# Turning the exponentials of local attention one step later, with the engines' orders moved to match

## The reference

```
q, k, v = split(shift_token(x) @ wqkv)
q = l2norm(q) * qs ; k = l2norm(k) * ksc ; q, k = rotary_xpos(q, k)
sim = einsum(q * 8, look_around(k))          # 64 queries against 128 keys
sim = where(i < j or i > j + 64 or j == -1, -max, sim)
o = softmax(sim) @ look_around(v)
x = x + o @ wo
h = layernorm(shift_token(x)) * lg + lb
a, g = split(h @ w1 + b1) ; x = x + (a * gelu(g)) @ w2 + b2
```

## Time and profile before

| | |
|---|---|
| median of 3 runs | 1146.2 us (1145.76 to 1147.83) |
| the profiled execution | 1146.11 us, of which its span 1144.2 |
| granted TensorE clock, mean | 0.978 of full speed |
| TensorE busy | 1070.0 us, 94% of the span |
| VectorE busy | 836.6 us, 73% |
| ScalarE busy | 632.1 us, 55% |
| GpSimd busy | 751.2 us, 66% |

### The profile page before, as it was taken

One profiled execution on the slowest core, in us unless ns is written; L12 is line 12 of the kernel. 1 busy time (PEld: TensorE's weight loads), 2 busy tenths in 40 slices (PEclk: granted clock), 3 DMA queues, 4 the chain that ended last, 5 costly groups with the idle time before them and its releaser, 6 DMA issues. The chain is left out here.

```text
span 1144.2 us, 22954 instructions
## 1 busy us (share of the span) xinstructions
PE 1070.0 (94%) x8344; PEld 665.8 (58%) x8344; DVE 836.6 (73%) x1521; ACT 632.1 (55%) x998; POOL 751.2 (66%) x511
## 2 busy tenths in 40 slices
PE   6884899999999999999999999789999898999988
PEld 4452455555555555555555555756777795777678
DVE  6994666666766666676666663889998689888867
ACT  2442356666666566656655654036666455666554
POOL 3662466767677776867677677389996337666526
PEclk9996799999999999999999999899999999999999
DMA  8899621524215243151242101001111100111111
GB/s 260 275 270 352 155 54 48 111 71 88 75 47 113 48 91 84 50 116 43 75 94 66 48 11 47 10 10 32 42 33 32 26 2 19 32 33 33 34 26 36
DMA packets 82625, 88.48 MB, mean 77 GB/s; under 512 B 32037, under 2 KB 65361, under 8 KB 82513
## 3 DMA queue, kind: packets, MB, share of 16 engines
q1 hardware_dynamic: 82512, 87.01, 29.7%
HBM read 53.04 MB, written 24.24 MB: 68 GB/s over the span
## 5 line engine op out<-in xcount | busy, mean ns | idle before, releaser
L873 DVE CUSTOM_DVE_ANT_0 junk<-psum,alibi 128x1024 bf16<-128x1024 f32 x256 | 313.1, 1223 | 200.7 <-PE psum L929 191.9
L845 ACT ACTIVATE E<-psum,keybias_sb 128x1024 f32<-128x1024 f32 x256 | 274.7, 1112 | 229.0 <-PE psum L953 215.8
L775 POOL TENSOR_TENSOR sum_p<-sum_p,E 128x1024 f32<-128x1024 f32 x96 | 232.4, 2421 | 89.3 <-ACT E L845 84.6
L965 PE MATMUL psum<-E,V 128*64 128x512 f32 x1024 | 248.2, 606 | 0.0
L929 PE MATMUL psum<-KH,QH 64*128 64x512 f32 x512 | 118.8, 459 | 12.8 <-PEq L274 7.3
L965 PEld LDWEIGHTS psum<-E,V 128*64 128x64 f32 x1024 | 62.2, 136 | 112.2 <-issue 98.5
L781 POOL TENSOR_TENSOR sum_p<-sum_p,xpos_sb 128x1024 f32<-128x1024 f32 x32 | 76.3, 2383 | 69.1 <-DVE xpos_sb L883 69.1
L929 PEld LDWEIGHTS psum<-KH,QH 64*128 64x128 f32 x512 | 49.5, 189 | 121.8 <-DVE M L873 84.5
L953 PE MATMUL psum<-QH,KH 64*128 64x512 f32 x512 | 102.3, 395 | 2.1 <-DVE M L873 2.1
L953 PE MATMUL psum<-QL,KH 64*128 64x512 f32 x512 | 101.7, 392 | 0.0
L953 PE MATMUL psum<-QH,KL 64*128 64x512 f32 x512 | 101.6, 392 | 0.0
(11 more groups left out here) (151 smaller groups left out, 2079.3 us busy)
## 6 DMA issues: line engine op xcount, KB each, us to landing
QH<-qa_scratch SPq DMA_DIRECT2D x64, 256.0 KB, 4.2
qa_scratch<-tH SPq DMA_DIRECT2D x8, 1024.0 KB, 5.4
qa_scratch<-tL SPq DMA_DIRECT2D x8, 1024.0 KB, 7.8
QL<-qa_scratch SPq DMA_DIRECT2D x64, 128.0 KB, 4.1
vp_att<-v_att SPq DMA_DIRECT2D x64, 128.0 KB, 2.3
XF<-inverse_scratch SPq DMA_DIRECT2D x30, 256.0 KB, 3.5
KH<-k_scratch SPq DMA_DIRECT2D x16, 256.0 KB, 4.1
KL<-k_scratch SPq DMA_DIRECT2D x16, 256.0 KB, 5.3
```

The lines of the kernel that those rows point to most:

```text
L775: pool.tensor_tensor(sum_p[:, s, :], first, E[:, k % 4, :], ALU.add)\
L845: act.activation(E[:, k % 4, :], scores(k % 2), ACT.Exp, bias=kb).then_inc(exp_done, 1)
L873: dve.tensor_tensor_reduce(junk[:, :], banks(max_bank(i, k), 2), alibi[:, s, :], -1.0, BIG, ALU.add, ALU.min, M[:, s, k:k + 1]).then_inc(m ...
L965: last = pe.matmul(banks(6 + i % 2)[HD * ch:HD * ch + HD, :], V[:, g, k, :], E[:, k % 4, ch * 512:(ch + 1) * 512], start=(k == 0), stop=(k ...
```

## The change

In the local attention `turn_e` and `take_eT` move from lag SCORES to lag PV: a tile's exponentials are turned in the next step, between the scores and the value projection of the next tile. The lists of ScalarE, VectorE and TensorE are put into a new order. `multiply_v` takes even heads first, then odd ones. The waits on the turned exponentials are counted for the new lag. The MLP swaps its bank pairs: even tiles use banks 5 and 6, odd ones 3 and 4.

```diff
 scalar
-        return [(square, NORMS), (take_v, SCORES), (exponentials, SCORES), (take_eT, SCORES), (take_oT, PV),
-                (take_qkT, TURN_QK), (take_hT, TURN_X)]
+        return [(square, NORMS), (take_eT, PV), (take_v, SCORES), (exponentials, SCORES), (take_qkT, TURN_QK),
+                (take_oT, PV), (take_hT, TURN_X)]
 vector
-        return [(maxima, SCORES), (normalise, TURN_QK), (weighted, PV), (square_sums, NORMS), (products, PROJECT),
-                (denominators, SCORES), (residual, OUT)]
+        return [(maxima, SCORES), (normalise, TURN_QK), (square_sums, NORMS), (weighted, PV), (products, PROJECT),
+                (residual, OUT), (denominators, SCORES)]
 tensor
-            for h in range(FH):
+            for h in (*range(0, FH, 2), *range(1, FH, 2)):
                 need(pe, eT_done, 2 * t + slot(h) // 4 + 1)
...
         def turn_e(t, s):
             need(pe, exp_done, t + 1)
-            need(pe, qkT_done, 2 * (t + 1))
+            need(pe, qkT_done, 2 * min(t + 2, T))
...
-                need(pe, eT_done, 2 * (t - 1) + n + 1)
+                need(pe, eT_done, 2 * (t - 2) + n + 1)
...
-        return [(multiply_qk, SCORES), (multiply_v, PV), (project_v, SCORES), (shift_scores, SCORES),
-                (project_qk, PROJECT), (turn_e, SCORES), (turn_o, PV), (turn_qk, TURN_QK), (project_out, OUT),
-                (turn_x, TURN_X)]
+        return [(multiply_qk, SCORES), (turn_e, PV), (project_v, SCORES), (shift_scores, SCORES), (multiply_v, PV),
+                (project_qk, PROJECT), (turn_qk, TURN_QK), (turn_o, PV), (project_out, OUT), (turn_x, TURN_X)]
 gated_mlp
-        return banks(3 + 2 * s)[:, HC * P:(HC + 1) * P]
+        return banks(5 - 2 * s)[:, HC * P:(HC + 1) * P]
...
-            if t < 2:
-
+            if t == 0:
+                pe.wait_ge(before["exp_done"], T)
+            if t == 1:
                 pe.wait_ge(before["eT_done"], 2 * T)
-                pe.wait_ge(before["exp_done"], T)
```

More of the change, by code:

```diff
@@ L1592, in gelu @@
             for j, n in enumerate(width):
-                act.activation(gate[0:n, s, j, :], banks(3 + 2 * s)[0:n, j * P:(j + 1) * P], ACT.Gelu,
+                act.activation(gate[0:n, s, j, :], banks(5 - 2 * s)[0:n, j * P:(j + 1) * P], ACT.Gelu,
                                bias=fb_1[0:n, l, 1, j:j + 1]).then_inc(gelu_done, 1)
@@ L1626, in gated @@
                 need(dve, gelu_done, HC * t + j + 1)
-                dve.scalar_tensor_tensor(act_in[0:n, s, j, :], banks(4 + 2 * s)[0:n, j * P:(j + 1) * P],
+                dve.scalar_tensor_tensor(act_in[0:n, s, j, :], banks(6 - 2 * s)[0:n, j * P:(j + 1) * P],
                                          fb_1[0:n, l, 0, j:j + 1], gate[0:n, s, j, :], ALU.add, ALU.mult)\
@@ L1654, in hidden @@
                 for j, n in enumerate(width):
-                    last = pe.matmul(banks(3 + 2 * s + m)[0:n, j * P:(j + 1) * P],
+                    last = pe.matmul(banks(5 - 2 * s + m)[0:n, j * P:(j + 1) * P],
                                      fw_1[:, l, off + j * P:off + j * P + n], hT[:, s, :],
```

## The result

The changed kernel takes 1151.6 us, the median of six runs (1149.2 to 1153.2), where the kernel before takes 1146.5 beside it: a ratio of 1.004, 95% interval 1.0027 to 1.0054. It is slower by 0.4%, past the 0.2% that can be told from no change. The forecast had said 1147.4 and "same"; the median of these runs lies 0.1 us above the range's end of 1151.5, and the ratio applied to the 1146.2 that was shown gives 1150.8, inside it. The profiled execution took 1151.6 with a span of 1149.7, against 1146.1 and 1144.2 before: 5.5 us to find.

The account below looks back on a forecast made before the run. TensorE, busy throughout full steps, was taken to bound the kernel, with waits at layer ends. Entries, full steps and exits summed to +0.5 and +0.8 us in the two layers, +1.3 on 1146.1: 1147.4 us, range 1144.0 to 1151.5.

Parts of the forecast that it names:

- Full steps: Ten full steps in a layer: each grows from 8.99 to 9.11 us, +1.2 us per layer.
- TensorE's own 8.98: Full step, TensorE by itself: 8.99 less 0.16 of wait for turned exponentials, plus 0.15 for a passage between array forms.
- the wait for bank 7: Full step: `turn_x` waits for ScalarE's copy of the turned outputs, 2.32 against TensorE's own 2.20, so 0.12 us late.
- VectorE as the bound: Rival: VectorE's residual chain delays maxima, full steps grow 0.15 more, 4 us more in all, 1151.4; slower cases together 0.30.
- Entries: Steps 4 and 5 of a layer: shorter by 1.1 us in the first layer and 0.8 in the second.
- Steps 17 and 18: Near a layer's end: step 17 takes 7.3 us, a change of -1.25; step 18 takes 7.5, a change of -1.0.
- The exit: Scores of step 19 to the MLP's first hidden product: 14.35 us instead of 11.7 to 11.8, +2.6 per layer.
- +0.4 per layer: Steps 16 to 20 together: -1.25 and -1.0 in steps 17 and 18, +2.6 from step 19 to the MLP.
- the 0.30 for "slower": Whole kernel: chance 0.30 of a result slower than can be told from no change, beyond 1148.5 us.

Follow-up runs that it names:

- the second experiment: Changed kernel, but TensorE turns the outputs, and ScalarE copies them, ahead of queries and keys again in every step: 1151.5 us, ratio 1.0035 to the kernel before.
- the first experiment: Changed kernel, but VectorE computes the softmax denominators ahead of the residual again: 1143.9 us, ratio 0.9966 to the kernel before.
- the version with both orders undone: Changed kernel with denominators ahead of the residual, and outputs turned and copied ahead of queries and keys, everywhere: 1143.2 us, ratio 0.9972 to the kernel before.
- the first try at filling it: Changed kernel plus five unused matmuls before the MLP's first transpose, placed behind the wait for the normalised input: 1155.8 us, ratio 1.0073 to the kernel before.

## Why the prediction failed at the exit and held elsewhere

**Full steps.** TensorE's own 8.98 (8.99 - 0.16 + 0.15) was right to 0.01: the second experiment shows 8.98 with the wait for bank 7 gone. The wait itself was there, for ScalarE's copy of the outputs, but it cost 0.18 and not the 0.12 to 0.13 of the sum. From the queries' transposes to `turn_x` the changed kernel needs 2.36 where the sum had 2.32, and `turn_x`, having waited, starts with cold weights (0.30 for 0.27). The ten steps grew by 1.5 and 1.8 us where +1.2 was forecast, 0.3 and 0.6 too little. Here the timelines of TensorE and ScalarE in the full step:

```profile
819.97 1.04 PE L1485 MATMUL psum<-ident,qk_att 128*128 128x128 f32 x8
820.85 0.60 PE L1470 MATMUL psum<-ident,O_att 128*128 128x128 f32 x4
821.28 1.06 PE L1494 MATMUL psum<-fw_o,oT_att 128*128 128x128 f32 x8
822.33 0.30 PE L1447 MATMUL psum<-ident,XF 128*128 128x128 f32 x1
...
820.61 0.60 ACT L1306 ACTIVATE qT_att<-psum 128x512 f32<-128x512 f32 x1 [2.35 <-PE psum L1485]
821.10 0.59 ACT L1310 ACTIVATE kT_att<-psum 128x512 f32<-128x512 f32 x1
821.58 0.61 ACT L1316 ACTIVATE oT_att<-psum 128x512 f32<-128x512 f32 x1
```

The outputs' copy ends at 822.19, and L1447 starts 0.14 later, as in the earlier trace rows. The profile puts no releaser at L1447, because the busy time of L1494 is modelled past its start; the wait shows only as 1.05 from L1494 where the earlier trace rows have 0.89.

**VectorE as the bound** was a rival, and it did not come: the maxima follow the reciprocal without idle time, but TensorE never waits for the shift in a full step, and the order of the first experiment leaves the step at 9.16. GpSimd, on which that rival also rested, stretched nothing in the chain: in full steps the products took 0.68 each before and after, the maxima 1.22. Only `normalise` (L1343) varied, from 1.25 to 2.30 before and from 1.22 to 1.93 after, with the same shape each time, and no wait of TensorE for it shows; what stretches it was not tried.

**Entries.** -1.1 and -0.8 forecast, -1.0 and -0.8 measured, with step 4 at the 6.80 that was reckoned. In the first layer that is partly luck: it needed a granted clock of 1.00 in step 4, which eight other profiled executions did not have (last section).

**Steps 17 and 18.** 7.3 and 7.5 forecast, 7.26 and 7.45 measured.

**The exit** is the term that failed: +2.6, and with the gains of steps 17 and 18 "+0.4 per layer". Measured is +4.5 and +3.6, which makes +2.2 and +1.2. The chain of waits in it was right: 14.35 forecast, 14.26 measured with the idle time filled. The term that was missing is TensorE's clock behind the wait. The working left out that a chain of waits empties TensorE, and that it then may do the rest at the lower level. It had laid down that the transpose comes only at 9.45, but priced every instruction behind at the durations of the earlier trace rows, all read at a granted clock of 1.00. The lower level cost 2.0 and 1.0 us in the exits of the profiled execution and went on into the MLP. By the medians, filling the idle time moves the ratio from 1.0040 to 1.0018, 2.5 us, though the intervals touch and the two ran in different groups.

Without it the changed kernel would have been at 1148 to 1149, near the 1147.4 forecast. So what made it slower beyond what can be told from no change is a cost that none of the cases held: neither the range nor the 0.30 for "slower" was built on it. The case that came nearest in time, VectorE as the bound at 1151.4, is by its steps not what happened, and that the range built on it reaches to the result is luck.

Of the change itself the runs give this account, per layer. Turning the exponentials a step later, read from the version with both orders undone, pays 0.1 us (with step 4 partly at the lower level) and 0.7 at the two entries and 1.1 in steps 17 and 18. It costs nothing on balance in full steps, where the extra passage eats the wait that goes, and 0.9 at the exit (12.6 for 11.7), where the last tile's are turned late; turned in their own step they give that back. Of the 2.9 us between the profiled spans of the kernel before and the version with both orders undone, these stages make 1.7, full steps included, and the end of the first layer's MLP nearly all the rest, through the granted clock (last section); how much of that the move brings is open. Outputs copied last gain 1.7 in steps 17 and 18 and lose 1.8 in full steps. The residual ahead of the denominators gains nothing anywhere and loses 3.2 in the exits, nearly half of it by the clock, and 0.5 in steps 17 and 18.

## What to carry to other kernels

When a change lets an engine run dry at the end of a stage, price the instructions behind the gap twice, at full and at half clock, and put the second into the range: here an order that made the idle time 1.3 us longer cost 1.7 us in waits and up to 2.0 more at the lower level. Judge an order by stages, since the best order of the full steps need not be that of the first and last ones: dividing one function at a tile number gave both gains, where either order alone gave one. And of a reordering that moves several things, try each alone: here the change was 0.4% slower than the kernel before, and 0.3% faster with two of its reorderings left out.

## What the runs showed of the hardware

The clock's response is not the same from one place or execution to the next. The idle time of 2.15 us was followed by the lower level after 1.6 us in the first layer of the changed kernel, and at once in the second (0.50 from the MLP's first transpose on). In the first try at filling it, with the same work behind it in both layers, the lower level came almost at once in the second layer and not at all in the rest of the first layer's exit. Counted over the profiled executions: of four unfilled exits with 2.15 us of idle time (the changed kernel, the second experiment) three ran partly at the lower level; of fourteen with 0.83 or less, the filled ones among them, one did, the first layer's in the kernel with the added passage, 13.06 us at 0.90. So in these few exits the long idle time mostly brought the fall, and was neither sure to bring it nor needed for it. Nor does it need an edit to differ: step 4 of the first layer took 6.80 us at a granted clock of 1.00 in the changed kernel, and 7.67 at 0.84 in the version with filled idle time, whose code is the same there.

```profile
761.07:767.87 6.80, 5.88 (x52) 3.36 (x52) 5.63 (x7) 3.03 (x6) 3.53 (x5) 1.00 0.17 39
761.50:769.17 7.67, 6.97 (x53) 4.27 (x52) 5.63 (x7) 3.04 (x6) 3.09 (x4) 0.84 0.15 34
```

The first row is the changed kernel, the second that version. The lower level fell into this step in eight of the ten profiled executions, the one with the added passage in the kernel before among them (9.29 us at 0.82). The kernel before and the changed kernel are the two without it, so the -1.0 at the first layer's entry compares like with like. The end of the MLP does the same: 12.0 us at 0.86 in the kernel before, and 1.00 throughout in the first experiment, whose stretch from the first hidden product to the second layer's scores is 49.4 us against 50.8. Together that is some 2 us, within the 2 to 5 us by which the runs of one kernel differ; what decides which level is granted in these two places was not tried.

A passage of TensorE between forms of the array together with the cold weights behind it costs 0.19 to 0.20 us in each of steps 5 to 16, in which it was added, and does not show as idle time: TensorE is busy for all of the 9.18 us of a full step. In steps 17 and 18, where TensorE waits for others anyway, each grew by 0.14.
